# Image loop rewritten as a six-stage software pipeline, second layer norm applied by VectorE

## Chip, cores and metric

One core of one Trainium2 chip. The metric is the device time of one launch in microseconds (us), the median of three runs. Engines: TensorE (PE; its weight loads are PEld), VectorE (DVE), ScalarE (ACT), GpSimd (POOL), and SyncE (SP), which issues the DMAs of the loop.

## The reference, cut to what matters

The input is 32 images of 96 channels by 28x28 positions, all float32.

```python
t0 = x + conv_experts(group_norm(x))   # gate picks 2 of 4 experts; relu(x w1 + b1) w2 + b2, weighted
t1 = t0 + attention(ln(t0))            # per 16-token window: A = fk^T fv * gauss * (1 - lambda), out = q A
y  = t1 + ffn(ln(t1))                  # bitlinear -> gelu -> bitlinear, signs as weights
def bitlinear(x, W, b):                # 5 groups of the batch, each scaled by its own largest |y|
    y = einsum('btc,oc->bto', x, sign(W - mean)) + b
    return clip(y * 128 / (max|y of the group| + 1e-5), -128, 128)
```

The names of the sketch are shortened; attention is linear (no softmax): exp of keys and values gives the feature maps fk and fv, summed into a 96x96 matrix A. The feed-forward part works on 30 of the 32 images (five groups of six).

## The kernel before, in words

Four stages follow one another: statistics and gating (all images resident in SBUF), the image loop, the scales of the first feed-forward layer, and the gelu/second-layer loop, which also writes the result. The change rewrites the second stage.

An image is 96 x 784; it is handled as 7 chunks of 112 tokens. Four PSUM slots S[0] to S[3] of two banks each are shared by everything. Each engine has a program of its own, in a fixed order, and runs it in that order; engines wait for one another by semaphores alone. In the loop a step `i` holds three images: the experts of image i, the attention of image i-1, the first feed-forward layer of image i-2.

TensorE's order in a step (function `step` in the tensor block, L1064): `hidden` 0 and 1 (L1009, 18 matmuls in f16 parts for the three tiles), transposes of t2T(i-2) to tokens (L877), `hidden` 2, transposes of tok1(i-1) to channels, `mix` (L1025, experts' second layer), `kv` (L1070), transposes of the normalised tok2(i-2) to channels, transposes of t1cm(i) to tokens, the sum A of fk and fv (L1173), `ffn_tile` 0, two small matmuls (L1184, L1186), `ffn_tile` 1, a small matmul (L1196), `ffn_tile` 2 (L1032/L1035), and the attention's output (L1202).

VectorE (L1479): statistics of tok2 (`stats`, L1438/L1445), t1cm (L1519), the two feature maps (L1485), the low half of the feed-forward input (`lo`, L1527), the mask Am (L1434), statistics of tok1, three `absmax` over feed-forward tiles (L1457), t2T (L1543), and `apply` (L1451), which normalises tok1 in seven instructions. ScalarE moves PSUM to SBUF (relu L767, tokens L761, xh1T L792, exp L774, big L798) and normalises the next image. GpSimd computes 1/sqrt of the variances (`rstd`, L603 and L609), the low part of the normalised image (`xn_lo`, L583, after it has waited for `xh1_ready`, that is for VectorE's apply), and normalises tok2 (L616). `keep_busy` (L941) are matmuls whose result nobody reads.

In the data of this run both experts' flags agree, so the branch `If(mixed)` takes its `Else` side (L1519) on every image.

Of the kernel before, what the change touches and what calls it, by code (L numbers as in the profile page):

```python
# [7 lines left out]
ALU = mybir.AluOpType  # L8
# [21 lines left out]
P = 128  # L30
# [95 lines left out]
def build(nc, x, gate_w, gate_b, w1, b1, w2, b2, qkv_w, qkv_b, proj_w, proj_b,  # L126
          lk1, lv1, lk2, lv2, W1, fb1, W2, fb2, consts, out):
    with ExitStack() as ctx:
# [24 lines left out]
        w1_raw = sb("w1_raw", [P, TILES, C])  # L153
        w2_raw = sb("w2_raw", [C, E, C])
# [57 lines left out]
        two_ones = sb("two_ones", [PARTS, HALF])  # L212
# [35 lines left out]
        ln_nm = sb("ln_nm", [TOK, CHUNKS])  # L248
# [13 lines left out]
        gel = hT  # L262
# [26 lines left out]
        pool_passed = sem("pool_passed")  # L289
# [54 lines left out]
        xs_loaded = [sem(f"xs_loaded{r}") for r in range(2)]  # L344
        xn_ready = sem("xn_ready")
# [3 lines left out]
        z_ready = sem("z_ready")  # L349
        h_ready = sem("h_ready")  # L350
# [3 lines left out]
        tmp_ready = sem("tmp_ready")  # L354
# [5 lines left out]
        ln_stats = sem("ln_stats")  # L360
# [3 lines left out]
        ln2_negated = sem("ln2_negated")  # L364
# [4 lines left out]
        kv_ready = sem("kv_ready")  # L369
        e_ready = sem("e_ready")  # L370
        f_ready = sem("f_ready")
# [13 lines left out]
        y_ready = sem("y_ready")  # L385
        ymax_done = sem("ymax_done")
# [40 lines left out]

        def piece_of(b):
            return max(n for n, first in enumerate(X_PIECES) if first <= b)
# [5 lines left out]
        def _(sp):  # L435
# [21 lines left out]
            load(fb1r[C:C + PARTS, :], fb1.rearrange("(a n) -> a n", a=1).to_broadcast([PARTS, HID]))  # L457
# [4 lines left out]
            for r in range(2):  # L462
                sp.dma_start(xs[r][:, :], x_bcn[r]).then_inc(xs_loaded[r], 16)

            def load_next(m, r):
                sp.wait_ge(t1_ready, 2 * m + r + 1)
                sp.dma_start(xs[r][:, :], x_bcn[2 * m + r + 2]).then_inc(xs_loaded[r], 16)

            def store_last(m, r):
                i = 2 * m + r  # L470
                sp.wait_ge(t2_ready, i)
                sp.dma_start(out_bcn[i - 1], t2T[1 - r][:, :]).then_inc(t2T_stored[1 - r], 16)

            for m in range(FIRST // 2):
                for r in range(2):
                    load_next(m, r)
                    if m + r > 0:
                        store_last(m, r)
            with sp.Fori(FIRST // 2, LAST // 2 - 1) as m:
                for r in range(2):  # L480
                    load_next(m, r)
                    store_last(m, r)
            for r in range(2):
                store_last(LAST // 2 - 1, r)
            store_last(LAST // 2, 0)
# [38 lines left out]
        def _(pool):  # L524
# [43 lines left out]
            def bf16_parts(src, rows, width, masks):  # L568
                b, h, c = part_b[rows, 0:width], part_h[rows, 0:width], part_c[rows, 0:width]
# [4 lines left out]
            def bf16_rest(dst, rows, width, masks):  # L574
                b, h, c = part_b[rows, 0:width], part_h[rows, 0:width], part_c[rows, 0:width]
# [18 lines left out]
            bf16_parts(fb1r[rows, :], rows, HID, con[rows, K_PART96:K_PART96 + 2])  # L594
            gn_power(4)
            bf16_rest(W1b[rows, :], rows, HID, con[rows, K_PART96:K_PART96 + 2])
# [4 lines left out]
            def rstd(n, b):  # L601
# [3 lines left out]
                if n == 1:  # L605
                    nc.gpsimd.tensor_scalar(ln_nm[:, :], ln_mv[n][:, :, 0], -1.0, None,
                                            ALU.mult).then_inc(ln2_negated, 1)
# [4 lines left out]
            def normalize_2(b):  # L612
                wait_apart(pool, ln_rstd[1], b + 1, pool_passed)
                wait_apart(pool, ln2_negated, b + 1, pool_passed)
                for j in range(CHUNKS):
                    ins = nc.gpsimd.tensor_scalar(tok2[:, j, :], tok2[:, j, :], ln_nm[:, j:j + 1],  # L616
                                                  ln_rs[1][:, j:j + 1], ALU.add, ALU.mult)
                ins.then_inc(xh2_ready, 1)

            def step(m, r, next_=True):  # L620
                i = 2 * m + r
                if next_:
                    pool.wait_ge(xh1_ready, i)
                    xn_rest(1 - r, i + 1)
                if not isinstance(i, int) or i >= 2:
                    rstd(1, i - 2)
                    normalize_2(i - 2)
                rstd(0, i)

            step(0, 0, next_=False)  # L630
            step(0, 1)
            with pool.Fori(1, LAST // 2 - 1) as m:
                for r in range(2):
                    step(m, r)
            step(LAST // 2 - 1, 0)
            step(LAST // 2 - 1, 1, next_=False)
# [3 lines left out]
        def _(act):  # L640
# [99 lines left out]
            def norm_image(m, r, i):  # L740
                resident = isinstance(i, int) and i < FIRST
                if not resident:
                    act.wait_ge(xs_loaded[r], 16 * (m + 1))
                if isinstance(i, int):
                    wait_count(act, z_ready, 3 * (i - 1))
                    wait_count(act, xn_lo_ready, i - 1)
                else:
                    wait_apart(act, z_ready, 3 * (i - 1), act_passed)
                    wait_apart(act, xn_lo_ready, i - 1, act_passed)
                source = x_all[:, i, :] if resident else xs[r][:, :]  # L750
                nc.scalar.activation(xn[r][:, :], source, ACT.Identity, scale=gn_scale[:, bass.ds(i, 1)],
                                     bias=gn_shift[:, bass.ds(i, 1)]).then_inc(xn_ready, 1)
                wait_apart(act, xn_ready, i + 1, act_passed)
                nc.scalar.copy(xn_hi[r][:, :], xn[r][:, :]).then_inc(xn_hi_ready, 1)
# [906 lines left out]
```

## Time and profile before

| what | value |
|---|---|
| time, median of 3 runs (lowest, highest) | 833.73 us (830.05, 836.1) |
| the profiled execution's own time | 830.4 us |
| its span, first to last instruction | 828.6 us |
| mean granted TensorE clock | 0.979 |
| busy: PE, DVE, ACT, POOL | 764.3, 585.8, 476.6, 272.6 us |

The image loop runs from the first `hidden` at 66.97 us to the first gelu at 657.82 us; the last stage, where ScalarE is busy 38.10 of 40 us, takes the rest. In the timeline a row is a run of instructions of one line: start, time to the end of the last, engine, line, operands and in brackets how long the engine idled before and what ended it. An instruction's end overlaps the next one's start, so the time that a piece of work takes up on its engine is read from start to start.

### The profile page before, as it was taken

How to read it: one execution, taken by the hardware profiler on the slowest of the kernel's cores; microseconds unless marked ns; L12 is line 12 of the kernel's file. 1: busy time of each engine (PE TensorE's matmuls, PEld its weight loads, DVE VectorE, ACT ScalarE, POOL GpSimd, SP SyncE). 2: the span in 40 equal slices, each digit the busy share in tenths (PEclk: the TensorE clock that was granted, in tenths of full speed). 3: DMA queues.
4: the chain of work that ended last, by engine and by line, in shares of the span. 5: the costliest groups of instructions: out<-in, count | busy, mean ns of one | idle time of the engine just before them, and what ended most of it. 6: DMA issues, size and time to landing. Idle time of an engine off the chain costs nothing.

```text
span 828.6 us, 15226 instructions
## 1 busy us (share of the span) xinstructions
PE 764.3 (92%) x4663; PEld 508.1 (61%) x4663; DVE 585.8 (71%) x1735; ACT 476.6 (58%) x684; POOL 272.6 (33%) x449
## 2 busy tenths in 40 slices
PE   6798889999999999999999999999999999999991
PEld 3465566667666667666666776666766555555540
DVE  3576467766777766777766677776677468999997
ACT  2453445545555554545554555554553499988981
POOL 1350244454344455334455434345433000000000
PEclk8899999999999999999999999999999999999996
DMA  9860001111111110101100101111100101463333
GB/s 216 198 149 16 22 24 45 31 29 36 36 29 29 44 29 29 44 29 29 43 29 29 44 29 29 32 41 29 34 24 15 32 28 54 150 176 114 119 117 116
DMA packets 20351, 48.62 MB, mean 59 GB/s; under 512 B 4937, under 2 KB 5223, under 8 KB 20327
## 3 DMA queue, kind: packets, MB, share of 16 engines
q1 hardware_dynamic: 19928, 47.72, 20.9%
q10 hardware_dynamic: 399, 0.60, 0.3%
q8 instruction: 13, 0.21, 0.1%
q14 instruction: 11, 0.09, 0.0%
HBM read 29.51 MB, written 18.67 MB: 58 GB/s over the span
## 4 chain that ended last, share of the span: by engine, by line
PE 69%; DVE 10%; ACT 7%; issue 7%; SPq 3%; POOL 2%; DMA 1%; DVEq 0%; ACTq 0%; POOLq 0%
PE slot L1025 15%; PE slot L1009 9%; PE slot L1032 7%; PE slot L1035 6%; PE slot L1173 5%; PE slot L1070 5%; PE slot L1202 5%; PE slot L1233 4%; PE slot L877 4%; PE slot L1237 4%; DVE stage L1485 3%; ACT stage L774 3%; SPq L445 3%; ACT hT L767 2%; PE slot L941 1%
## 5 line engine op out<-in xcount | busy, mean ns | idle before, releaser
L1025 PE MATMUL slot<-hT,w2s 128*96 128x392 f32 x384 | 134.0, 499 | 2.9 <-ACT hT L767 2.3
L774 ACT ACTIVATE stage<-slot,minus_one 112x768 f32<-112x768 f32 x64 | 52.5, 821 | 125.7 <-PE slot L1070 123.3
L767 ACT ACTIVATE hT<-slot,b1c,w_unit 128x784 f32<-128x784 f32 x96 | 93.1, 1006 | 23.0 <-PE slot L1009 23.0
L1519 DVE SCALAR_TENSOR_TENSOR t1cm<-slot,bias,xs 96x784 f32<-96x784 f32 x32 | 32.9, 1029 | 96.9 <-PE slot L1025 96.9
L1025 PEld LDWEIGHTS slot<-hT,w2s 128*96 128x96 f32 x384 | 60.0, 163 | 63.0 <-issue 53.6
L609 POOL TENSOR_TENSOR ln_rs<-ln_ve,pow_half 112x7 f32<-112x7 f32 x62 | 92.8, 1497 | 2.5
L1032 PE MATMUL slot<-big,W1b 99*128 (+1 forms) x360 | 89.5, 329 | 2.7 <-DVE big L1527 0.8
L1035 PE MATMUL slot<-big,W1b 96*128 (+1 forms) x360 | 89.2, 328 | 0.0
L616 POOL TENSOR_SCALAR tok<-tok,ln_nm,ln_rs 112x96 f32<-112x96 f32 x210 | 84.9, 421 | 9.2 <-POOL ln_rs L609 9.2
L583 POOL TENSOR_TENSOR xn_lo<-xn,xn_hi 96x784 f16<-96x784 f32 x32 | 54.4, 1701 | 101.5 <-DVE tok L1451 101.5
L831 ACT ACTIVATE hT<-slot,s 128x784 f32<-128x784 f32 x90 | 80.3, 926 | 6.6 <-DVE stage L1567 6.3
L603 POOL TENSOR_TENSOR ln_ve<-ln_mv,ln_eps 112x7 f32<-112x7 f32 x62 | 12.6, 204 | 216.7 <-DVE ln_mv L1445 216.7
L1457 DVE TENSOR_REDUCE ymax<-slot 128x784 f32 (+1 forms) x90 | 81.2, 959 | 0.0
L1070 PEld LDWEIGHTS slot<-qkvw,xh1T 97*112 97x112 f32 x448 | 73.6, 177 | 10.5 <-issue 9.5
L1485 DVE SCALAR_TENSOR_TENSOR stage<-stage,slot 112x768 f32<-112x768 f32 x64 | 51.8, 850 | 40.0 <-ACT stage L774 40.0
L1070 PE MATMUL slot<-qkvw,xh1T 97*112 97x192 f32 x448 | 78.3, 326 | 0.1
L1438 DVE BATCH_NORM_STATS2 ln_st<-tok 112x6 f32<-112x96 f32 x434 | 74.9, 243 | 4.4 <-ACT tok L761 2.3
L1567 DVE SCALAR_TENSOR_TENSOR stage<-hT,stage 128x784 f16<-128x784 f32 x60 | 56.6, 968 | 14.5 <-ACT stage L840 14.5
L761 ACT COPY tok<-slot 112x672 f32<-112x672 f32 x62 | 44.5, 718 | 24.5 <-PE slot L877 24.5
L1451 DVE TENSOR_SCALAR tok<-tok,ln_mv,ln_rs 112x96 f32<-112x96 f32 x224 | 56.2, 323 | 1.9 <-POOL ln_rs L609 1.9
L1173 PE MATMUL slot<-stage 112*96 112x96 f32 x448 | 46.0, 255 | 12.3 <-DVE stage L1485 12.3
L877 PE MATMUL slot<-con,tok 112*96 112x112 f32 x434 | 52.8, 262 | 4.4 <-POOL tok L616 3.8
(192 smaller groups left out, 1344.6 us busy)
## 6 DMA issues: line engine op xcount, KB each, us to landing
out<-t2T SPq DMA_DIRECT2D x56, 294.0 KB, 2.6
xs<-in_x SPq DMA_DIRECT2D x32, 294.0 KB, 2.9
big<-in_x SPq DMA_DIRECT2D x7, 1176.0 KB, 16.1
xs<-out SPq DMA_DIRECT2D x24, 294.0 KB, 3.3
big<-out SPq DMA_DIRECT2D x1, 1764.0 KB, 11.9
out<-big SPq DMA_DIRECT2D x6, 294.0 KB, 2.6
big<-in_x SPq DMA_DIRECT2D x2, 588.0 KB, 24.3
con<-shape_consts ACTq DMA_DIRECT2D x1, 445.5 KB, 6.1
```

The costliest lines, as they stand in the source:

```text
L609: nc.gpsimd.tensor_tensor(ln_rs[n][:, :], ln_ve[n][:, :], pow_half[0:TOK, 0:CHUNKS], ALU.pow).then_inc(ln_rstd[n], 1)
L616: ins = nc.gpsimd.tensor_scalar(tok2[:, j, :], tok2[:, j, :], ln_nm[:, j:j + 1], ln_rs[1][:, j:j + 1], ALU.add, ALU.mult)
L767: nc.scalar.activation(hT[:, t, :].rearrange("p (a n) -> p a n", a=2), halves(t, P), ACT.Relu, scale=w1_unit[:, t:t + 1], bias=b1c[:, t:t ...
L774: nc.scalar.activation(ekv[:, j0:j0 + n, :], chunks(k, n, 256, 2 * C), ACT.Exp, bias=minus_one[:, :]).then_inc(e_ready, 1)
L831: nc.scalar.activation(gel[:, t, :].rearrange("p (a n) -> p a n", a=2), halves(t, P), ACT.Gelu, scale=s1[:, bass.ds(g, 1)]).then_inc(gelu_ ...
L877: return mm(o, i, ident[0:rows, 0:rows], start=start, stop=True, is_transpose=True, skip_group_check=True)
L1025: ins = mm(S[k][0:C, h, 0:HALF], w2s[:, v, t, :], hT[:, t, h * HALF:(h + 1) * HALF], start=t == 0, stop=t == TILES - 1, skip_group_check=True)
L1032: mm(S[k][:, h, 0:HALF], w, big[:, f, 0, h * HALF:(h + 1) * HALF], start=True, stop=False, skip_group_check=True)
L1035: ins = mm(S[k][:, h, 0:HALF], w[0:C, :], big[0:C, f, 1, h * HALF:(h + 1) * HALF], start=False, stop=True, skip_group_check=True)
L1070: ins = mm(chunks(k, n, 256, 2 * C)[:, j, :], xh1T[:, (j0 + j) * TOK:(j0 + j + 1) * TOK], qkvw[:, C:3 * C], start=True, stop=True, skip_gr ...
L1173: ins = mm(S[3][0:C, 0, 0:C], fkv[:, j, 0:C], fkv[:, j, C:2 * C], start=j == 0, stop=j == CHUNKS - 1)
L1457: V.tensor_reduce(ymax[:, bass.ds(3 * f + t, 1)], halves(k, P), AX.XY, ALU.max, apply_absolute_value=True).then_inc(ymax_done, 1)
```

## The change

The loop's steps now hold six images. A lag tells which image a part of the step works on: hidden layer i, experts' second layer i-1, attention's first half i-2, its second half i-3, tok2 i-4, feed-forward i-5. There are 34 steps after `first_hidden` instead of 32 and one. hT has two buffers, the residual input has its own (xr beside xs), and the setup's raw weights lie in the second hT buffer. GpSimd's `normalize_2` is gone; VectorE does it in the last instructions of its step.

```diff
+        LAG_NORM = LAG_HID = 0
+        LAG_MIX = 1
+        LAG_ATT = 2
+        LAG_OUT = 3
+        LAG_TOK2 = 4
+        LAG_FFN = 5
+        DRAIN = QIMAGES + LAG_FFN
...
@@ GpSimd
-            def normalize_2(b):
...
+            def step(m, r):
+                i, q, _ = at(m, r, LAG_ATT)
+                if exists(i):
+                    rstd(0, i)
+                i, q, _ = at(m, r, LAG_NORM)
+                if exists(i) and not (isinstance(i, int) and i < 2):
+                    xn_rest(q, i)
+                i, q, _ = at(m, r, LAG_TOK2)
+                if exists(i, QIMAGES):
+                    rstd(1, i)
...
@@ TensorE, the order of a step
+                    to_tokens(2, t2T[tok2_q], tok2_in_psum)
...
+                    wait_count(pe, ymax_done[1], ffn)
+                    pe.wait_ge(xh2_ready, ffn + 1)
+                    to_channels(0, tok2, x2p_ready)
...
+                    mix(1, 1, mix_q, 0, 2, 0).then_inc(y_mixed, 1)
...
+                    pe.wait_ge(xh1_ready, att + 1)
                     to_channels(0, tok1, x1T_ready)
...
+                    pe.wait_ge(xn_lo_ready, hid + 1)
+                    wait_count(pe, tok2_ready, tok2_image + 1)
+                    hidden(0, 2, hid_q)
...
+                    kv(0, 0, 0, CH_A)
...
+                    ffn_tile(ffn, 0, 1).then_inc(y_ready[0], 1)
...
+                    to_tokens(2, t1cm[mix_q], tok1_in_psum)
...
+                    kv(1, 3, CH_A, CHUNKS - CH_A)
...
+                    ffn_tile(ffn, 2, 1).then_inc(y_ready[2], 1)
...
+                    hidden(2, 2, hid_q)
...
+                    ffn_tile(ffn, 1, 0).then_inc(y_ready[1], 1)
...
@@ VectorE, the end of a step, the first and the last steps
+                if exists(ffn, QIMAGES):
+                    absmax(ffn, 2, 1)
+                    absmax(ffn, 1, 0)
+                if exists(tok2_image, QIMAGES):
+                    apply(1, tok2, tok2, tok2_image, xh2_ready)
+
+            dve.wait_ge(w0_ready, 1)
+            first_weights_in(1)
+            step(0, 1)
+            first_shares(1)
+            step(1, 0)
+            step(1, 1)
+            first_weights(1)
...
+            for i in range(BATCH, DRAIN):
+                step(i // 2, i % 2)
+            y1_max()
```

Where the instructions stand now, at three places.

TensorE, from the end of one loop step into the next, as changed (L1032 `hidden`, L1055/L1058 `ffn_tile` 1, L1227 the sum A, L900 transposes, L1152/L1153 small matmuls):

```order
L1032 MATMUL slot2<-xn_hi0,w1_lo 128x392 x2
L1055 MATMUL slot0<-big,W1b 128x392 [waits f_ready0]
L1055 MATMUL slot0<-big,W1b 128x392
L1058 MATMUL slot0<-big,W1b 128x392 x2
L1227 MATMUL slot3<-stage 96x96 [waits f_ready1,f_ready0]
L1227 MATMUL slot3<-stage 96x96 x6
L900 MATMUL slot2<-con,t2T1 112x96 [waits t2_ready,h_ready2]
L900 MATMUL slot2<-con,t2T1 112x96 x6
L900 MATMUL slot0<-con,tok2 96x112 [waits xh2_ready,ymax_done1]
L900 MATMUL slot0<-con,tok2 96x112 x6
L1152 MATMUL slot3<-wqT,Am 96x97 [waits am_ready]
```

Between the last feed-forward tile of a step and the transposes of tok2 there now stand the sum A and one set of transposes. Before, the same transposes stood behind `mix` and `kv`, and three tiles came later in the step.

VectorE, the end of a loop step and the start of the next, as changed (L1482 `absmax`, L1476 `apply`, L1547 the mask Am):

```order
L1507 SCALAR_TENSOR_TENSOR stage<-stage,slot3 112x576 [waits e_ready1]
L1482 ISA [waits y_ready2]
L1482 TENSOR_REDUCE ymax<-slot1 128x1
L1482 ISA [waits y_ready1]
L1482 TENSOR_REDUCE ymax<-slot0 128x1
L1476 TENSOR_SCALAR tok2<-tok2,ln_mv1,ln_rs1 112x96 [waits ln2_rstd]
L1476 TENSOR_SCALAR tok2<-tok2,ln_mv1,ln_rs1 112x96 x6
L1547 TENSOR_TENSOR Am<-slot3,gauss 96x96 [waits a_ready]
```

The seven instructions on tok2 stand behind the `absmax` that reads the step's last feed-forward tile, and ahead of the next step's mask and statistics.

GpSimd, one loop step before (first fence) and as changed (second):

```order
L583 TENSOR_TENSOR xn_lo0<-xn0,xn_hi0 96x784 [waits xn_hi_ready]
L603 TENSOR_TENSOR ln_ve1<-ln_mv1,ln_eps 112x7 [waits ln2_mean]
L606 TENSOR_SCALAR ln_nm<-ln_mv1 112x7
L609 TENSOR_TENSOR ln_rs1<-ln_ve1,pow_half 112x7 [waits ln2_var]
L616 TENSOR_SCALAR tok2<-tok2,ln_nm,ln_rs1 112x96 [waits ln2_rstd,ln2_negated]
L616 TENSOR_SCALAR tok2<-tok2,ln_nm,ln_rs1 112x96 x6
L603 TENSOR_TENSOR ln_ve0<-ln_mv0,ln_eps 112x7 [waits ln1_mean]
L609 TENSOR_TENSOR ln_rs0<-ln_ve0,pow_half 112x7 [waits ln1_var]
```

```order
L634 TENSOR_TENSOR ln_ve0<-ln_mv0,ln_eps 112x7 [waits ln1_mean]
L637 TENSOR_TENSOR ln_rs0<-ln_ve0,pow_half 112x7 [waits ln1_var]
L614 TENSOR_TENSOR xn_lo1<-xn1,xn_hi1 96x784 [waits xn_hi_ready]
L634 TENSOR_TENSOR ln_ve1<-ln_mv1,ln_eps 112x7 [waits ln2_mean]
L637 TENSOR_TENSOR ln_rs1<-ln_ve1,pow_half 112x7 [waits ln2_var]
```

xn_lo follows the power of the first norm directly and no longer waits for `xh1_ready`; VectorE's apply on tok1 waits for that same power.

## Rows read from the trace of the kernel before

**Rows 1.** Windows: busy us (instructions) of PE, PEld, DVE, ACT, POOL; granted clock; DMA.
```profile
592.00:632.00 40.00, 39.12 (x239) 26.79 (x237) 27.57 (x106) 20.60 (x28) 17.74 (x29) 1.00 0.10 30
```
**Rows 2.** Timeline of PE, one step: start, us to the end, line, idle before.
```profile
588.04 1.48 PE L1202 MATMUL slot<-xh1T,R 97*96 97x392 f32 x4
589.36 0.50 PE L1009 MATMUL slot<-xn_hi,w_hi 96*128 96x392 f16 x2
...
591.35 0.74 PE L877 MATMUL slot<-con,t2T 96*112 96x96 f32 x7
591.93 0.49 PE L1009 MATMUL slot<-xn_hi,w_hi 96*128 96x392 f16 x2
...
592.92 0.84 PE L877 MATMUL slot<-con,tok 112*96 112x112 f32 x7
593.81 4.19 PE L1025 MATMUL slot<-hT,w2s 128*96 128x392 f32 x12
597.83 2.44 PE L1070 MATMUL slot<-qkvw,xh1T 97*112 97x192 f32 x14
600.11 0.84 PE L877 MATMUL slot<-con,tok 112*96 112x112 f32 x7
600.78 0.74 PE L877 MATMUL slot<-con,t1cm 96*112 96x96 f32 x7
601.94 1.43 PE L1173 MATMUL slot<-stage 112*96 112x96 f32 x14 [0.42 <-DVE stage L1485]
603.38 0.50 PE L1032 MATMUL slot<-big,W1b 99*128 x2
...
604.05 0.33 PE L1184 MATMUL slot<-wqT,Am 96*96 96x97 f32 x2
...
605.89 1.48 PE L1202 MATMUL slot<-xh1T,R 97*96 97x392 f32 x4
```
**Rows 3.** Timeline of DVE in the same step.
```profile
598.04 1.03 DVE L1519 SCALAR_TENSOR_TENSOR t1cm<-slot,bias,xs 96x784 f32<-96x784 f32 x1 [3.21 <-PE slot L1025]
600.27 1.62 DVE L1485 SCALAR_TENSOR_TENSOR stage<-stage,slot 112x768 f32<-112x768 f32 x2 [1.21 <-ACT stage L774]
...
603.41 0.26 DVE L1434 TENSOR_TENSOR Am<-slot,gauss 96x96 f32<-96x96 f32 x1 [0.29 <-PE slot L1173]
...
605.43 2.71 DVE L1457 TENSOR_REDUCE ymax<-slot 128x784 f32 x3
608.05 0.96 DVE L1543 TENSOR_TENSOR t2T<-slot,t1cm 96x784 f32<-96x784 f32 x1
608.93 1.75 DVE L1451 TENSOR_SCALAR tok<-tok,ln_mv,ln_rs 112x96 f32<-112x96 f32 x7
```
**Rows 4.** Timeline of POOL in the same step: the power of the first norm.
```profile
605.88 1.48 POOL L609 TENSOR_TENSOR ln_rs<-ln_ve,pow_half 112x7 f32<-112x7 f32 x1
```
**Rows 5.** Line L583 by itself: shortest, median and longest in ns, first and last start.
```profile
L583 POOL TENSOR_TENSOR xn_lo<-xn,xn_hi x32: 1664/1675/2491, 24.3 to 610.8; 96x784 f16<-96x784 f32 x32
```
**Rows 6.** Timeline of POOL and DVE around the longest L583.
```profile
103.88 0.61 DVE L1334 TENSOR_REDUCE stage<-stage 112x112 f32<-112x448 f32 x1
104.13 2.49 POOL L583 TENSOR_TENSOR xn_lo<-xn,xn_hi 96x784 f16<-96x784 f32 x1 [2.24 <-DVE tok L1451]
...
104.70 0.38 DVE L1336 TENSOR_TENSOR stage<-stage 112x224 f32<-112x224 f32 x1
...
105.89 0.87 DVE L1338 TENSOR_TENSOR stage<-stage 112x112 f32<-112x112 f32 x1
...
107.78 0.27 DVE L1343 TENSOR_TENSOR stage<-stage 112x112 f32<-112x112 f32 x1
```
**Rows 7.** Timeline of PE, two places in the first steps.
```profile
79.66 0.79 PE L877 MATMUL slot<-con,t1cm 96*112 96x96 f32 x7 [1.12 <-DVE t1cm L1519]
...
115.10 1.52 PE L877 MATMUL slot<-con,tok 112*96 112x112 f32 x7 [3.07 <-POOL tok L616]
```
**Rows 8.** Timeline of ACT: the first two gelus.
```profile
657.82 1.89 ACT L831 ACTIVATE hT<-slot,s 128x784 f32<-128x784 f32 x2
```

More of the change, by code:

```diff
@@ L344, in build @@
         xs_loaded = [sem(f"xs_loaded{r}") for r in range(2)]
+        xr_loaded = [sem(f"xr_loaded{r}") for r in range(2)]
         xn_ready = sem("xn_ready")
@@ L479, in _, with load_norm @@
[L479 to L485, printed above, removed]
+                sp.dma_start(xr[r][:, :], x_bcn[r]).then_inc(xr_loaded[r], 16)
+            for r in range(2):
+                sp.dma_start(xs[r][:, :], x_bcn[FIRST + r]).then_inc(xs_loaded[r], 16)
+            def load_norm(m, r):
+                i, q, _ = at(m, r, LAG_NORM)
+                if not isinstance(i, int) or FIRST <= i < BATCH - 2:
+                    sp.wait_ge(xn_ready, i + 1)
+                    sp.dma_start(xs[q][:, :], x_bcn[i + 2]).then_inc(xs_loaded[q], 16)
@@ L486, in _ @@
+            def step(m, r):
+                load_norm(m, r)
+                store_t2(m, r)
+                load_residual(m, r)
+            for i in range(EVEN_FIRST):
+                step(i // 2, i % 2)
+            with sp.Fori(EVEN_FIRST // 2, BATCH // 2 - 1) as m:
+                for r in range(2):
+                    step(m, r)
+            for i in range(BATCH - 2, DRAIN):
+                step(i // 2, i % 2)
             for r in range(2):
@@ L817, in _ @@
+            relu(0, 0, 0, 0)
+            gate_exps(0, 1)
+            relu(0, 0, 2, 2)
+            relu(1, 1, 0, 0)
+            relu(0, 0, 1, 1)
+            relu(1, 1, 1, 2)
+            relu(1, 1, 2, 0)
+            act.wait_ge(signs_ready, 1)
+            nc.scalar.copy(W2last[:, :], W2b[:, TILES - 1, :])
+            gate_exps(1, 0)
+            for i in range(1, EVEN_FIRST):
+                step(i // 2, i % 2)
                 if i == 2:
                     gate_exps(1, 1)
-            with act.Fori(FIRST // 2, LAST // 2 - 1) as m:
+            with act.Fori(EVEN_FIRST // 2, BATCH // 2) as m:
@@ L820, in _ @@
                 for r in range(2):
                     step(m, r)
[L822 to L824 removed]
+            for i in range(BATCH, DRAIN):
+                step(i // 2, i % 2)
             def gelu_tile(g, b, t):
@@ L1170, in step @@
-                if attend:
-                    pe.wait_ge(f_ready, 2 * i)
+                if exists(mixes):
+                    expert_differences(mixes, mix_q, 1)
+                if exists(hid) and not ahead:
+                    pe.wait_ge(xn_lo_ready, hid + 1)
+                    wait_count(pe, tok2_ready, tok2_image + 1)
+                    hidden(0, 2, hid_q)
+                    wait_count(pe, t2_ready, done + 1)
+                    if isinstance(hid, int) and hid == 2:
+                        pe.wait_ge(gate_exp_in, 3)
+                    hidden(1, 3, hid_q)
@@ new lines, in step @@
+                if exists(att):
+                    wait_count(pe, t2_ready, done + 1)
+                    wait_count(pe, h_ready[1], hid + 1 if exists(hid) else BATCH)
+                    kv(1, 3, CH_A, CHUNKS - CH_A)
+                if exists(ffn, QIMAGES):
+                    pe.wait_ge(ymax_done[0], ffn + 1)
+                    ffn_tile(ffn, 2, 1).then_inc(y_ready[2], 1)
+                if exists(hid) and not ahead:
+                    pe.wait_ge(tok1_ready, mixes + 1)
+                    hidden(2, 2, hid_q)
@@ L1556, in _ @@
+            dve.wait_ge(w0_ready, 1)
[5 more added lines that the diff above has]
+            first_weights(1)
+            for i in range(4, EVEN_FIRST):
+                step(i // 2, i % 2)
+            with dve.Fori(EVEN_FIRST // 2, BATCH // 2) as m:
                 for r in range(2):
                     step(m, r)
-            for r in range(2):
-                step(LAST // 2 - 1, r)
-            step(LAST // 2, 0, experts=False, ffn=False, scales=True)
+            for i in range(BATCH, DRAIN):
+                step(i // 2, i % 2)
```

644 lines of the change are left out of this document (296 added, 348 removed).

## The prediction, written before the changed kernel was timed

> **What bounds the kernel now.** I read the windows first, to see which engine is full in the image loop, then one step of TensorE, then VectorE and GpSimd in that step. In 40 us of the loop TensorE is busy for 39.12, VectorE for 27.57, ScalarE for 20.60 [rows 1]: TensorE sets the pace. The step from one attention output to the next takes 605.89 - 588.04 = 17.85 us [rows 2]. It holds two waits: the t1cm transposes take as long as the t2T ones, 0.58 (591.35 to 591.93), so TensorE stood from 601.36 to 601.94, 0.58; the tok transposes take 0.67 (600.11 to 600.78), so it stood 0.22 ahead of the mix at 593.81. The sum A with its wait behind it takes 1.44 (601.94 to 603.38). So some 16.9 to 17.05 us of a step is work, and perfect overlap could win 0.8 to 0.95 us a step, some 25 us in all. That is the prize. The question is whether the new order has a ring of waits that is as long as the old step.
>
> **The steady step after.** The matmuls of an image are the same, so TensorE's work is still 17.05 at most. At a step's start it does the t2T transposes, then the tok2 transposes, which wait for VectorE's apply on tok2, the last thing of the step before. That apply stands behind the absmax of `ffn_tile` 1, and this tile is TensorE's last piece but the sum A. So there is a ring: tok2 transposes, all of TensorE's step to the end of `ffn_tile` 1, absmax, apply, tok2 transposes again.
> - TensorE's part: 17.85 less the two waits (0.58 and 0.22), the sum A (1.44) and the t2T transposes (0.58): 15.03 [rows 2].
> - TensorE to VectorE: t1cm starts at 598.04, 0.21 after the next PE piece started at 597.83 [rows 2, 3].
> - absmax: three from 605.43 to 608.05, 0.87 each. apply: 1.75 to its end [rows 3]; tok2 has the shape of tok1.
> - VectorE to TensorE: the feature maps end at 601.89, PE starts at 601.94: 0.05.
>
> Sum: 15.03 + 0.21 + 0.87 + 1.75 + 0.05 = **17.91 us**. What covers the last four terms (2.88) is only the sum A and the t2T transposes, at most 2.02; the rest is a new wait of 0.9 or more a step. The two old waits do go: kv, transposes and two tiles now stand between the feature maps and their readers. One wait takes the place of two. Queued behind it on TensorE are the small matmuls, the mix and all of the step; ScalarE's St and VectorE's next waits come later by the same time, which the ring contains.
>
> A second ring runs through GpSimd. VectorE goes from the apply on tok2 to the mask Am and the statistics of tok1; from Am's start at 603.41 to the end of the power at 605.88 + 1.48 = 607.36 it is 3.95 [rows 3, 4]. Then apply on tok1 and xn_lo both become free to run. xn_lo, which used to wait for that apply, normally takes 1.68 [rows 5]. If apply goes first and xn_lo after it, xn_lo ends at 3.95 + 0.05 + 1.75 + 1.54 after Am's start (the 1.54 from the next paragraph), and `hidden` 0 waits for it. From `hidden` 0 to the end of `ffn_tile` 1 TensorE's part is 15.03 less the two tok transposes (1.34), the mix (4.02), the output (1.32) and the three small matmuls (603.38 to 605.89 less three tiles of 0.67: 0.50), so 7.85 [rows 2]. Ring: 7.85 + 0.21 + 0.87 + 1.70 (apply, to the next start) + 3.95 + 0.05 + 1.75 + 1.54 + 0.05 = 17.97. Both rings have the length of the old step, so I take **18.0 us** (17.9 to 18.1).
>
> Why 1.54: in the longest xn_lo, 2.49 from 104.13 to 106.62, VectorE ran two-operand operations until 104.70 + 0.38 = 105.08 at their usual length, and then one of 112 columns took 0.87, although one of 224 took 0.38, and ended as xn_lo did [rows 6]. They exclude each other; xn_lo had 1.54 left.
>
> Off the path: VectorE's busy time grows from 12.3 (27.57 x 17.85 / 40) to some 14 us a step, below 18; GpSimd loses its seven operations, which were hidden anyway. SyncE issues one load more per image (xs and xr); its store waits for t2 with the residual's load queued behind, but both loads are used two steps on. ScalarE's xn now heads its step, behind relu 2, and runs while TensorE waits and mixes, before xn_lo is due. These cost nothing while the step is 18 us.
>
> **Filling and draining.** Until the first t1cm transposes at 79.66 [rows 7] nothing that ends last is moved: the hidden layers of image 1 take the place of keep-busy matmuls. Mix 1 ends at 79.66 + 0.58 + 4.02 = 84.3. But `first_shares(1)` now stands ahead of the statistics of image 0: from 103.88 to 107.78 + 0.27 it took 4.2 with a stall of some 0.6 in it [rows 6], so 79.6 + 3.6 = 83.2; statistics and power 3.78 (3.95 less 0.17 for Am), apply 1.85: the tok1 transposes start at 88.9. TensorE has then idled 4.5 us; after 3.07 idle the next transposes took 1.52 where 0.84 is usual [rows 7, 2]. I add 1.4, twice what that set lost. Then 5.5 of PE work, the chain from kv over exp and feature maps to A (600.11 to 601.94, 1.83) and A (1.44): step 2 ends at 99.0. Steps 3 and 4 have no feed-forward and bare chains: 15.0 and 15.6. The tok2 transposes of step 5 start at 99.0 + 30.6 + 0.6 = 130.2. From there to those of step 32 it is 27 steps. The drain (steps 32 and 33 of some 15 us each, as chains lie bare without hidden layers, 10.5 for step 34, 4.3 for the scales, which now begin only after it) I put at 45; the matmuls alone make 28, full steps would make 58; 41 to 49 is my range.
>
> First gelu: 130.2 + 27 x 18.0 + 45 = 661.2, against 657.82 [rows 8]; with a possible slow restart in the drain (0 to 1.5) **+4 us**. At 17.9 and a drain of 41 it is -3, at 18.1 and 49 +10. The last stage is untouched. The profiled execution took 830.4 (span 828.6 and 1.8 around it), so it becomes 834.4. The median of the runs shown, 833.73, is 3.3 higher; on it the sum is **838**, its own range 831 to 843. A change of less than 1% (8.3 us) can't be told from none here.
>
> **The rivals.**
> *GpSimd first, slower.* xn_lo follows the power in GpSimd's own queue, while VectorE's apply must be released by that power. If xn_lo gets in first and apply waits 1.68 for it, apply ends at 3.95 + 1.68 + 1.75 = 7.4 after Am's start; the tok1 transposes would start 6.6 after it (7.18 of PE pieces less their own 0.67 and 0.1 that Am starts earlier). TensorE waits 0.8, the step is 18.7, and 27 steps cost 19 more: 857. It decides where apply is held up by more than 0.8. For it: GpSimd's release is the shorter. Against: VectorE operations that started 0.6 after xn_lo's recorded start were not held up [rows 6]. The Trainium skill, "SBUF — State Buffer", section "SBUF: two separate sides", says that VectorE and GpSimd share a port pair that is an "exclusive lock", and that whoever starts first holds it for the whole instruction. That both exclude each other the trace agrees with; by the rule taken literally GpSimd, first to start, would win here, and the time would be 857. Chance 0.24.
>
> *Small waits add up, slower.* Three chains of nearly one length meet in a step; if each hand-over costs 0.1 more than I read, or the clock falls in some steps, s is 18.25 to 18.4 and the time 844 to 848. It decides from 18.17. Chance 0.18, a quarter of it still within 1%.
>
> *The waits vanish, faster.* If absmax and apply were early enough, TensorE would run its 17.05: 27 x 0.95 = 26 less, 812. Against it stands the order: this absmax can't start before the tile is written. Chance 0.08; a run of before 3 us above the others doesn't help it.
>
> **How the numbers follow.** Forecast 0.50 (nearly all within 1%, 0.02 above). Slower: 0.24 + 0.14 + 0.02 = 0.40; within 1%: 0.48 + 0.04 = 0.52; faster 0.08. The range 830 to 857 leaves out the faster case and the tails.
>
> **What would show it.** In the profile after: steps of 17.9 to 18.1; TensorE idle 0.9 to 1.1 before the tok2 transposes, ended by VectorE's apply; no wait left before A or the mix; xn_lo of 2.5 to 3.3 where apply on tok1 runs (apply first) or an apply stretched by 1.6 (GpSimd first); an idle of over 4 us near 85; gelu from about 661. I am wrong if the tok2 transposes find xh2 ready, or if the step isn't within 17.9 to 18.1.

## The result, and the profile after

The changed kernel takes 863.69 us (862.03 to 865.37), the kernel before 834.78 beside it (830.05 to 836.1): a ratio of 1.0357 (95% interval 1.0307 to 1.0407), 29 us more. The forecast was 838, no change that can be told, with 857 as the upper end of the range.

The profiled execution took 862.03 (span 860.0). Windows of it; the first line answers to [rows 1], the others are the last steps of the image loop and the start of the feed-forward stage:

```profile
592.00:632.00 40.00, 37.06 (x240) 25.98 (x239) 33.73 (x106) 21.06 (x28) 10.00 (x10) 1.00 0.08 23
632.00:672.00 40.00, 31.81 (x180) 22.23 (x178) 29.84 (x110) 9.92 (x17) 6.72 (x8) 0.85 0.06 16
672.00:712.00 40.00, 36.23 (x146) 18.30 (x146) 19.53 (x27) 24.35 (x33) 0.00 (x0) 0.77 0.08 23
```

TensorE is busy 37.06 of 40 instead of 39.12, at full clock (2.4 GHz), so the loop waits more than before; later the granted clock falls to 0.85 and 0.77. In the windows from 632 to 712 of before it was 1.00.

TensorE at the start of two steps (the transposes of tok2, of tok1, of tok2 again; it answers to [rows 2]):

```profile
541.18 0.85 PE L900 MATMUL slot<-con,tok 112*96 112x112 f32 x7 [1.17 <-DVE tok L1476]
...
548.17 0.85 PE L900 MATMUL slot<-con,tok 112*96 112x112 f32 x7 [0.35 <-DVE tok L1476]
...
559.72 0.88 PE L900 MATMUL slot<-con,tok 112*96 112x112 f32 x7 [1.08 <-DVE tok L1476]
```

A step is 559.72 - 541.18 = 18.54 here, and 18.61 in the mean of the 27 from 131.86 (step 5) to 634.25 (step 32). TensorE stands 1.17 and 1.08 us by the rows ahead of the tok2 transposes, about as foreseen (0.9 to 1.1), and again ahead of the tok1 transposes, which was not: the mix's last piece starts at 546.33 and its like takes 1.32 from start to start, so it should have ended at 547.65, 0.5 before they start. (The row shows 0.35, since it counts from the recorded end of the mix, 1.48 after its start. Counted from start to start the two waits at tok2 are 1.33 and 1.24.)

VectorE and GpSimd in that step, answering to [rows 3, 4, 5] (L1482 absmax, L1476 both applies, L637 the power, L614 xn_lo):

```profile
537.39 1.97 DVE L1482 TENSOR_REDUCE ymax<-slot 128x784 f32 x2
539.28 1.76 DVE L1476 TENSOR_SCALAR tok<-tok,ln_mv,ln_rs 112x96 f32<-112x96 f32 x7
540.95 0.25 DVE L1547 TENSOR_TENSOR Am<-slot,gauss 96x96 f32<-96x96 f32 x1
...
543.40 1.48 POOL L637 TENSOR_TENSOR ln_rs<-ln_ve,pow_half 112x7 f32<-112x7 f32 x1
544.85 1.67 POOL L614 TENSOR_TENSOR xn_lo<-xn,xn_hi 96x784 f16<-96x784 f32 x1
...
544.92 3.11 DVE L1476 TENSOR_SCALAR tok<-tok,ln_mv,ln_rs 112x96 f32<-112x96 f32 x7 [0.55 <-POOL ln_rs L637]
```

xn_lo keeps its 1.67; the apply on tok1, released by the same power 0.07 later, takes 3.11 instead of 1.76. A narrow window on VectorE shows which of its seven instructions it is:

```profile
544.92 1.67 DVE L1476 TENSOR_SCALAR tok<-tok,ln_mv,ln_rs 112x96 f32<-112x96 f32 x1 [0.55 <-POOL ln_rs L637]
```

The first one alone lasts until xn_lo ends. That is the mechanism of the rival "GpSimd first".

Filling, answering to [rows 7]: the wait near 85 is there, the slow set behind it too.

```profile
77.32 0.79 PE L900 MATMUL slot<-con,t1cm 96*112 96x96 f32 x7 [1.21 <-DVE t1cm L1535]
87.60 1.54 PE L900 MATMUL slot<-con,tok 112*96 112x112 f32 x7 [5.53 <-DVE tok L1476]
```

TensorE from step 33 to the scales (L1172 the attention output, 1.48 at full clock; L964 nine matmuls on constants), and ScalarE's first gelu, which answers to [rows 8]:

```profile
651.46 0.85 PE L900 MATMUL slot<-con,tok 112*96 112x112 f32 x7 [1.46 <-DVE tok L1476]
...
654.27 2.93 PE L1172 MATMUL slot<-xh1T,R 97*96 97x392 f32 x4 [1.06 <-ACT R L810]
...
669.75 1.09 PE L900 MATMUL slot<-con,tok 112*96 112x112 f32 x7 [2.04 <-DVE tok L1476]
...
672.47 2.93 PE L1172 MATMUL slot<-xh1T,R 97*96 97x392 f32 x4 [0.33 <-ACT R L810]
...
682.15 4.04 PE L964 MATMUL slot<-ones_f,ones_b 128*112 128x512 bf16 x9
```
```profile
688.80 0.92 ACT L854 ACTIVATE hT<-slot,s 128x784 f32<-128x784 f32 x1 [14.87 <-PE slot L1058]
```

Behind these waits the same matmuls take twice as long (2.93 instead of 1.48), which is half clock (1.2 GHz). From the tok2 transposes of step 32 to the first gelu it is 54.55, not 45.

### The profile page after: what moved, and what is told of

Its sections match the earlier page's. It is cut to its first block, busy times and chain, and to the rows that moved or that the text cites. A ratio compares the mean times of both kernels' runs of the same rounds, so it can differ in the third digit from the quotient of the medians.

```text
span 860.0 us, 14841 instructions
## 1 busy us (share of the span) xinstructions
PE 764.2 (89%) x4624; PEld 500.3 (58%) x4624; DVE 680.5 (79%) x1945; ACT 480.5 (56%) x684; POOL 178.1 (21%) x209
## 4 chain that ended last, share of the span: by engine, by line
DVE 34%; PE 31%; issue 9%; ACT 6%; POOL 6%; DVEq 1%; ACTq 0%; POOLq 0%
DVE tok L1476 16%; PE slot L1089 8%; PE slot L1032 7%; PE slot L900 6%; DVE ymax L1482 6%; POOL ln_rs L637 5%; DVE ln_st L1466 4%; PE slot L1055 3%; ACT stage L788 3%; PE slot L1058 2%; DVE stage L1602 2%; DVE ln_mv L1470 2%; PE slot L1265 1%; PE slot L1269 1%; ACT hT L854 1%
## 5 line engine op out<-in xcount | busy, mean ns | idle before, releaser
L1476 DVE TENSOR_SCALAR tok<-tok,ln_mv,ln_rs 112x96 f32<-112x96 f32 x434 | 149.5, 414 | 19.4 <-POOL ln_rs L637 19.4
L1048 PE MATMUL slot<-hT,w2s 128*96 128x392 f32 x384 | 141.7, 493 | 0.0
L1482 DVE TENSOR_REDUCE ymax<-slot 128x784 f32 (+1 forms) x90 | 87.3, 972 | 43.3 <-PE slot L1058 42.6
L782 ACT ACTIVATE hT<-slot,b1c,w_unit 128x784 f32<-128x784 f32 x96 | 96.1, 1004 | 36.3 <-PE slot L1032 36.2
L813 ACT COPY xh1T<-slot 96x784 f32<-96x784 f32 x32 | 25.8, 807 | 160.6 <-PE slot L900 160.6
L900 PE MATMUL slot<-con,tok 112*96 112x112 f32 x434 | 54.9, 268 | 50.4 <-DVE tok L1476 50.4
L1055 PE MATMUL slot<-big,W1b 99*128 (+1 forms) x360 | 91.9, 337 | 1.9 <-DVE ymax L1482 1.1
L637 POOL TENSOR_TENSOR ln_rs<-ln_ve,pow_half 112x7 f32<-112x7 f32 x62 | 91.8, 1480 | 4.8
L1058 PE MATMUL slot<-big,W1b 96*128 (+1 forms) x360 | 91.4, 335 | 0.0
L1089 PE MATMUL slot<-qkvw,xh1T 97*112 97x192 f32 x448 | 85.6, 332 | 1.8 <-ACT xh1T L813 1.8
L900 PEld LDWEIGHTS slot<-con,tok 112*96 112x96 f32 x434 | 41.6, 128 | 76.1 <-issue 40.7
L1507 DVE SCALAR_TENSOR_TENSOR stage<-stage,slot 112x768 f32<-112x768 f32 x64 | 54.3, 850 | 22.8 <-ACT stage L788 22.7
L1055 PEld LDWEIGHTS slot<-big,W1b 99*128 99x128 bf16 x360 | 35.1, 99 | 32.0 <-issue 13.2
L614 POOL TENSOR_TENSOR xn_lo<-xn,xn_hi 96x784 f16<-96x784 f32 x32 | 53.4, 1668 | 0.0
L1265 PE MATMUL slot<-stage,W2b 128*96 128x392 f16 x240 | 46.6, 334 | 5.9 <-DVE stage L1602 2.0
```

The lines of the kernel that those rows point to most:

```text
L637: nc.gpsimd.tensor_tensor(ln_rs[n][:, :], ln_ve[n][:, :], pow_half[0:TOK, 0:CHUNKS], ALU.pow).then_inc(ln_rstd[n], 1)
L782: nc.scalar.activation(hT[q][:, t, :].rearrange("p (a n) -> p a n", a=2), halves(k, P), ACT.Relu, scale=w1_unit[:, t:t + 1], bias=b1c[:, t ...
L900: return mm(o, i, ident[0:rows, 0:rows], start=start, stop=True, is_transpose=True, skip_group_check=True)
L1048: ins = mm(S[k][0:C, h, 0:HALF], w2s[:, v, t, :], hT[q][:, t, h * HALF:(h + 1) * HALF], start=t == first, stop=t == last, skip_group_check ...
L1055: mm(S[k][:, h, 0:HALF], w, big[:, f, 0, h * HALF:(h + 1) * HALF], start=True, stop=False, skip_group_check=True)
L1058: ins = mm(S[k][:, h, 0:HALF], w[0:C, :], big[0:C, f, 1, h * HALF:(h + 1) * HALF], start=False, stop=True, skip_group_check=True)
```

## The experiments

The fill is the loop's first steps, in which not all six images are there yet; the drain is its last ones. Three theories went in. T1: xn_lo holds up the apply on tok1, and the ring through the apply on tok2 comes on top. T2: the longer apply lies in slack, only the ring counts. T3: six images in flight cost by themselves. T4 to T6 came with the later runs. All ratios are to the kernel before, on the same chip. Per profile: the mean step (tok2 transposes of step 5 to step 32, over 27), and the drain (from there to the first gelu):

| run | us | ratio | step | drain |
|---|---|---|---|---|
| the change | 863.7 | 1.0357 | 18.61 | 54.6 |
| e1_xnlo_first | 936.3 | 1.1278 | 21.34 | 53.7 |
| e2_xnlo_waits | 856.6 | 1.0303 | 18.37 | 54.6 |
| e3_apply_mid | 846.6 | 1.0184 | 18.12 | 46.1 |
| e4_pool_norm2 | 817.1 | 0.9846 | 17.14 | 46.2 |
| e5_xnlo_gap | 845.9 | 1.0145 | 18.08 | 53.0 |
| e6_apply_early | 842.4 | 1.0106 | 18.06 | 48.9 |
| e7_busy_drain | 860.0 | 1.0320 | 18.61 | 54.2 |
| e8_pool_gap | 802.7 | 0.9635 | 16.76 | 45.6 |
| e9_busy_all | 856.7 | 1.0312 | 18.61 | 46.2 |
| e10_best | 800.1 | 0.9632 | 16.76 | 43.0 |
| e11_apply_behind_maps | 830.7 | 0.9988 | 17.43 | 54.9 |
| e12_fill_order | 801.4 | 0.9637 | 16.76 | 43.1 |

The start of the loop differs between profiles by some 4 us (the first t1cm transposes from 77.32 to 81.72), so steps and drains tell more than sums.

**e1_xnlo_first.** xn_lo ahead of the power in GpSimd's step.
```diff
+                xn_rest(q, i)          # first in the step
                 rstd(0, i)
-                xn_rest(q, i)
```


> Only GpSimd's order in a step changes: xn_lo ahead of the first norm's power instead of behind it. Theory 1 (GpSimd takes the shared access first and holds up VectorE's apply on tok1, so that TensorE waits 0.5 us a step before the tok1 transposes): apply 1.75 us instead of 3.11, no wait before these transposes, the step 18.6 becomes 18.05, that is 27 x 0.55 = 15 us less than the changed kernel's 863.7: about 849. Theory 2 (the longer apply lies in VectorE's slack and the step is set by absmax and the apply on tok2 alone): apply is shorter, but the wait only moves, the step stays 18.6 and the time 862 to 865.

936.3, interval of the ratio 1.1232 to 1.1323: a miss of both. xn_lo moved into the other apply. VectorE, GpSimd and TensorE there:

```profile
424.21 3.27 DVE L1476 TENSOR_SCALAR tok<-tok,ln_mv,ln_rs 112x96 f32<-112x96 f32 x7
425.51 1.66 POOL L614 TENSOR_TENSOR xn_lo<-xn,xn_hi 96x784 f16<-96x784 f32 x1 [7.39 <-ACT xn_hi L771]
...
427.63 0.95 PE L900 MATMUL slot<-con,tok 112*96 112x112 f32 x7 [2.69 <-DVE tok L1476]
...
429.01 2.80 PE L1048 MATMUL slot<-hT,w2s 128*96 128x392 f32 x4
```

The apply on tok2 had run for 1.3 us when xn_lo came, and still it was held up. A narrow window shows its last two instructions:

```profile
425.40 2.08 DVE L1476 TENSOR_SCALAR tok<-tok,ln_mv,ln_rs 112x96 f32<-112x96 f32 x2
```

Five of the seven took 0.24 each; the sixth, recorded 0.11 ahead of xn_lo, lasts until xn_lo has ended. GpSimd gets into the middle of the series. This apply is the ring itself, and TensorE's wait grows to 2.69. Behind it TensorE runs at half clock (1.2 GHz) for a while: the mix's four matmuls that start at 429.01 take 2.80 instead of 1.48, and the granted clock of 392 to 432 is 0.87. So 1.5 us of hold-up became 2.7 a step. T2's "no effect" falls; the size was in neither theory.

**e2_xnlo_waits.** xn_lo waits for the apply on tok1, as before the change.
```diff
+                    pool.wait_ge(xh1_ready, i - 1)
                     xn_rest(q, i)
```


> xn_lo waits again for the apply on tok1, as in the kernel before the change. Theory 1: apply 1.75 us, xn_lo 1.67 behind it, ends 0.2 to 0.3 after the tok1 transposes, so hidden 0 waits 0.2 to 0.3 where the transposes waited 0.5: step 18.3, about 8 us less than the changed kernel, 856. Theory 2: step 18.6, no change, 862 to 865.

856.6, interval 1.0277 to 1.0329: as T1. The apply on tok1 is back at 1.77, but xn_lo, now behind it, is at the edge of what `hidden` 0 waits for (a wait of 0.15 in some steps, ended by xn_lo): a step of 18.37 shows half of the gain that e5 finds below.

**e3_apply_mid.** The apply on tok2 right behind t1cm, ahead of the first absmax.
```diff
                     convolved(mixes, mix_q, mix_pair, 1)
+                    apply(1, tok2, tok2, tok2_image, xh2_ready)
 ...
-                    apply(1, tok2, tok2, tok2_image, xh2_ready)   # was last
```


> VectorE's apply on tok2 moves from the end of its step to just behind t1cm; GpSimd stays as in the changed kernel. Theory 1: the ring through the last absmax and this apply (15.06 + 0.32 + 0.9 + 1.75 + 0.05) is gone; what is left is VectorE's own chain with the held-up apply on tok1 (3.1 us): about 17.9 a step, 27 x 0.7 = 19 us less, 845. Theory 2: the apply was the whole of it, TensorE is full again, step 17.0 to 17.2, about 40 less, 823.

846.6, interval 1.0145 to 1.0223: the time as T1. No wait is left at tok2, but a new one of 0.8 stands ahead of `ffn_tile` 2, because the first absmax is late:

```profile
549.93 0.51 PE L1055 MATMUL slot<-big,W1b 99*128 x2 [0.79 <-DVE ymax L1482]
```

That the time fits is partly luck: the steps give 13 us (18.61 to 18.12) and not 19, and the drain, which T1 did not count, gives 8.4.

**e4_pool_norm2.** All of the rewrite, but GpSimd normalises tok2 as before.
```diff
-                    apply(1, tok2, tok2, tok2_image, xh2_ready)   # VectorE
...
+                    normalize_2(i)                                # GpSimd, behind rstd(1, i)
```


> The rewritten loop with six images, but GpSimd normalises tok2 as before the change, and VectorE does not. Theory 1: neither ring is left (absmax to the tok2 transposes: 16.3; through xn_lo and apply on tok1: 16.9), TensorE is full, step 17.0 to 17.2, about 40 us less than the changed kernel: 822 to 826, below the 834.8 of the kernel before. Theory 3 (six images in flight cost by themselves, through fill, drain and more hand-overs): step 17.9 or more, 845 or more.

817.1, interval 0.981 to 0.9881: the step is T1's, and T3 falls. The tok2 transposes no longer wait:

```profile
544.89 0.84 PE L915 MATMUL slot<-con,tok 112*96 112x112 f32 x7
...
551.75 0.85 PE L915 MATMUL slot<-con,tok 112*96 112x112 f32 x7 [0.24 <-DVE tok L1491]
```

The time lies below T1's 822; the drain, which T1 did not count, is 8.3 shorter than the change's. Six images in flight are a gain of 1.5%; the norm on VectorE is what made the change slow.

**e5_xnlo_gap.** The change, with xn_lo between the two applies.
```diff
...
+                        pool.wait_ge(xh2_ready, i - LAG_TOK2)    # not in the first steps
+                    xn_rest(q, i)          # now ahead of rstd(0, i)
...
-                    xn_rest(q, i)          # was behind it
```


> The change as it is, but GpSimd computes xn_lo first in its step and waits for the end of VectorE's apply on tok2 before it, so that xn_lo lies between the two applies and falls into neither. Theory T1 (GpSimd's subtraction, started during or just ahead of an apply, holds it up by its own length): the apply on tok1 is back at 1.76 us, TensorE loses the 0.5 us ahead of the tok1 transposes, the steps fall from 18.6 to about 18.1 and the time from 862 to 847-852. Theory T2 (the longer apply lies in slack, the step is set by the apply on tok2 alone): 860-864, steps still 18.5 or more.

845.9, interval 1.0114 to 1.0176: as T1, below its 847. TensorE, VectorE and GpSimd:

```profile
548.30 0.88 PE L902 MATMUL slot<-con,tok 112*96 112x112 f32 x7 [1.08 <-DVE tok L1478]
...
548.40 1.67 POOL L614 TENSOR_TENSOR xn_lo<-xn,xn_hi 96x784 f16<-96x784 f32 x1 [8.00 <-DVE tok L1478]
...
552.14 1.77 DVE L1478 TENSOR_SCALAR tok<-tok,ln_mv,ln_rs 112x96 f32<-112x96 f32 x7 [0.38 <-POOL ln_rs L637]
```

Neither apply is held up, the wait at tok1 is gone, that at tok2 is left: 18.08 a step is the first ring bare (17.91 predicted), and 18.61 - 18.08 = 0.53 a step, 14 us in 27 steps, is the collision.

**e6_apply_early.** The apply on tok2 between the first absmax and the feature maps.
```diff
                     absmax(ffn, 0, 1)
+                    apply(1, tok2, tok2, tok2_image, xh2_ready)
                     feature_map(att, 0, 0, 0, CH_A)
...
-                    apply(1, tok2, tok2, tok2_image, xh2_ready)   # was last
```


> The change as it is, but VectorE applies the second layer norm between the first absmax of its step and the feature maps, not at the end. GpSimd's order is that of the change. Theory T1 (the wait is the place at the end of the step, behind absmaxes that end 2 us after TensorE): no idle time ahead of the tok2 transposes, steps near 17.2 and 818-826, as with the norm on GpSimd; what remains is the held-up apply on tok1, 0.2 us a step. Rival T4 (1.75 us more on VectorE is too much for it wherever it stands, and comes out at another wait, behind the feature maps or the second absmax, as it did 0.8 us a step when the apply stood ahead of the first absmax): steps near 18.0, 838-846.

842.4, interval 1.0074 to 1.0137: as T4. TensorE, the third tile and the tok1 transposes:

```profile
548.46 0.51 PE L1055 MATMUL slot<-big,W1b 99*128 x2 [0.49 <-DVE stage L1507]
...
557.88 0.88 PE L900 MATMUL slot<-con,tok 112*96 112x112 f32 x7 [0.23 <-DVE tok L1476]
```

The wait moved behind the feature maps, which come 1.7 later. The apply on tok1 is still held up (3.10), in e3 too, so the steps of these two runs hold the collision as well.

**e7_busy_drain** and **e9_busy_all.** Matmuls on constants where TensorE stands in steps 33 and 34: e7 ahead of the tok2 transposes, e9 at each wait.
```diff
+                if late:
+                    pe.wait_ge(ymax_done[2], hid - LAG_FFN)
+                    keep_busy(1, 0, 6)                       # e7 and e9
...
                     to_tokens(2, t2T[tok2_q], tok2_in_psum)
...
+                        keep_busy(1, 0, 5)                   # e9, then r_ready
...
+                        keep_busy(1, 0, 6)                   # e9, then xh1_ready
...
+                        keep_busy(1, 0, 4)                   # e9, then xh1T_ready
```


> The change as it is, but in each of the last four steps TensorE first does six matmuls of 512 columns on constants into a slot that nobody reads, where it now stands idle 1.1 to 2 us waiting for the apply on tok2. Theory T5 (TensorE's idle time in the drain is followed by half clock, and the half clock, not the waits themselves, makes the drain 54.5 us instead of 45): the rows of the drain are at full rate (the attention output 1.48 instead of 2.93), the first gelu comes 5-9 us earlier, 853-858. Rival T6 (the drain is long because its steps wait for VectorE, clock or no clock): 860-864.

> The change as it is, with the filling matmuls of the run before this one ahead of the tok2 transposes in the last steps, and now also 4 to 6 of them at each other wait of those steps (ahead of the attention output, of the tok1 transposes, of kv), so that TensorE hardly idles there. In the change the drain's last step ran at half clock and its rows are 5.6 us longer than the same rows of the version with the norm on GpSimd, which were at full clock. Theory T5 (idle time is followed by half clock, and that costs these 5 us): rows at full rate throughout, the drain 48-50 us instead of 54.5, total 856-860. Rival T6 (half clock or not, the waits set the drain): drain 53-55, 861-865.

The edits act in two steps, 33 and 34, not in the last four. e7: 860.0, interval 1.0267 to 1.0373, drain 54.2, as T6 had it; but part of its rows were still at half clock (the last group of matmuls took 4.04 again), so it told nothing yet. e9: 856.7, interval 1.0286 to 1.0339. TensorE in its drain:

```profile
658.54 1.56 PE L1178 MATMUL slot<-xh1T,R 97*96 97x392 f32 x4
...
674.15 1.48 PE L1178 MATMUL slot<-xh1T,R 97*96 97x392 f32 x4
...
680.82 2.11 PE L964 MATMUL slot<-ones_f,ones_b 128*112 128x512 bf16 x9
```

Full clock throughout, and a drain of 46.2 with more matmuls in it than 54.6 had: T5. Filling TensorE's idle time took 8.4 us off the drain. The whole time shows less of it: 856.7 after 863.7, but ratios of 1.0312 and 1.0357, whose intervals overlap. In the profiles e9's loop starts 4.4 later and its first gelu comes 4.1 earlier (684.67).

**e8_pool_gap.** e4, with xn_lo first in GpSimd's step.
```diff
+                xn_rest(q, i)          # first in the step
                 rstd(0, i)
-                xn_rest(q, i)
                 rstd(1, i)
                 normalize_2(i)
```


> The six-image loop with the second layer norm left on GpSimd (817 us in the run before), and xn_lo moved to the start of GpSimd's step, where VectorE has no apply. T1: the apply on tok1 falls from 3.1 to 1.76 us; TensorE waited for it only 0.24 us in every other step, so the steps go from 17.2 to about 17.1 and the time to 812-817. Against T1: no shorter apply, or xn_lo holds up the statistics on tok1 instead, 817-825.

802.7, interval 0.9605 to 0.9665: more than T1 gave it. Windows of TensorE, then VectorE and GpSimd:

```profile
512.00:552.00 40.00, 40.00 (x274) 29.57 (x273) 31.16 (x101) 24.18 (x32) 18.92 (x34) 1.00 0.18 51
```
```profile
551.91 1.67 POOL L617 TENSOR_TENSOR xn_lo<-xn,xn_hi 96x784 f16<-96x784 f32 x1 [3.69 <-ACT xn_hi L786]
...
555.34 1.76 DVE L1491 TENSOR_SCALAR tok<-tok,ln_mv,ln_rs 112x96 f32<-112x96 f32 x7 [0.74 <-POOL ln_rs L643]
```

TensorE never waits: 16.76 is the bare step. e4 lost 0.38 a step (17.14): counted from start to start, its tok1 transposes begin 0.3 to 0.4 late in each step, where the rows show 0.24 in every other one.

**e11_apply_behind_maps.** VectorE's best place found: behind the feature maps, ahead of two absmaxes in the other order, xn_lo first on GpSimd.
```diff
+                    apply(1, tok2, tok2, tok2_image, xh2_ready)
+                    absmax(ffn, 1, 0)
                     absmax(ffn, 2, 1)
-                    absmax(ffn, 1, 0)
-                    apply(1, tok2, tok2, tok2_image, xh2_ready)
```


> VectorE applies the second layer norm, but behind the feature maps and ahead of two absmaxes, whose order is exchanged, and xn_lo is first in GpSimd's step: neither apply is held up, and the tok2 transposes wait for the first of the two absmaxes alone. T1 (the loss is the place and the held-up apply): steps 17.0-17.5, 810-824. T4 (VectorE's 1.75 us more come out at whichever wait follows: statistics and apply on tok1 now start 1.4 us later, ahead of the tok1 transposes): steps 17.6-18.1, 826-842.

830.7, interval 0.9971 to 1.0006. The steps are T1's, 17.43; the time is T4's. Its drain of 54.9 ran at half clock again in part, and 8.7 us less there, as e9 had it, would bring the time into T1's range; no run filled this drain. Wherever VectorE's 1.75 us stood (e3, e5, e6, e11), the step stayed 0.7 to 1.4 above the bare one, in e3 and e6 with some of it due to the held-up apply on tok1.

**e10_best** and **e12_fill_order.** e8 with the gate shares later and the drain filled as in e9, except ahead of the tok2 transposes; e12 takes the power ahead of xn_lo while the loop fills.
```diff
-            first_shares(1)                      # ahead of step 2
...
+                    first_shares(1)              # in step 2, ahead of feature_map
...
 # e12, steps below EVEN_FIRST: xn_rest behind rstd(0, i) and the wait
+                    pool.wait_ge(xh1_ready, new - LAG_ATT + 1)
```


> The best version so far (six images in flight, second layer norm on GpSimd, xn_lo first in GpSimd's step; 802.7) with two more edits: the shares of the second half of the gates are worked out where VectorE waits 7 us for the first exponentials, not ahead of the first statistics, and the drain's waits are filled with matmuls. The first tok1 transposes come 3.5 us earlier and the rows behind them are less slowed (1-1.5): 4-5 us; the drain gains 2-3 where half clock is avoided. 795-799; if the fill's time comes back at a later wait of the filling steps, 800-803.

> The fastest version so far (six images in flight, second layer norm on GpSimd, xn_lo first in GpSimd's step, shares of the second half behind the first t1cm, drain filled; 800.1), with one edit: in the filling steps alone GpSimd takes the power first and xn_lo only when the apply on tok1 is done, since there xn_lo stood 1.0 to 1.7 us ahead of the power in the bare chain from statistics to tok1 transposes. If that chain is what the fill waits for, the first tok1 transposes come 1.7 earlier and three later ones about 1 each: 795-798. If xn_lo behind the apply is then late for the hidden layers, 799-801.

e10: 800.1, interval 0.9606 to 0.9657: the drain gave 2.5 as expected, the fill 0.5 instead of 4 to 5, so its second case. e12: 801.4, interval 0.9612 to 0.9663, 0.4 above its second case. By their ratios e8, e10 and e12 (0.9635, 0.9632, 0.9637) can't be told apart. TensorE in the fill, of e10 and of e12:

```profile
88.93 1.54 PE L915 MATMUL slot<-con,tok 112*96 112x112 f32 x7 [4.04 <-DVE tok L1500]
```
```profile
87.86 0.88 PE L919 MATMUL slot<-con,tok 112*96 112x112 f32 x7 [2.51 <-DVE tok L1504]
89.61 0.84 PE L1051 MATMUL slot<-xn_hi,w_hi 96*128 96x392 f16 x2 [0.88 <-POOL xn_lo L617]
```

In e10 xn_lo stood ahead of the power, in e12 it was late for the hidden layers: two chains end there nearly together, and shortening one left the wait to the other.

## Why the prediction was wrong

From 657.82 the first gelu went to 688.80, 31 us; predicted were 3.4 without the slow restart, 661.2. The 27.6 between:

- **The steady step, 18.0 predicted, 18.61 measured: 16.4 us.** The step that failed is "if apply goes first and xn_lo after it". GpSimd goes first: it starts 0.07 ahead and VectorE's first instruction ends with it, so the tok1 transposes are held up, as the rival "GpSimd first" had it. Its worth is shown by e5: 0.53 a step, 14.3 us. That the rival's step of 18.7 comes so near is partly luck: it put the wait at 0.8 on a ring of 17.91, and they are 0.53 on 18.08. Its time, 857, falls short of 863.7 because it has the drain wrong too. The chance was set wrongly, 0.24, on one look at [rows 6]: there VectorE's operations ran on beside a started xn_lo. There GpSimd was the one held off (2.49 for 1.67), here it never is (1.66 to 1.69 in all 32); what decides between the two when their recorded starts are 0.1 apart, no run here tells. By the Trainium skill, "SBUF — State Buffer", section "SBUF: two separate sides", whichever starts first, GpSimd or a VectorE operation that needs the shared ports, holds them for its whole instruction. The change agrees with it, taken literally: GpSimd started 0.07 ahead and won. In e1 the recorded starts speak against it: VectorE's sixth instruction, recorded 0.11 ahead of xn_lo, was the one held up, and there the measurement decides. That the hold goes by single instructions e1 bears out: a series of seven is broken into.
- **The first ring itself, 17.91 predicted, 18.08 in e5: 2 of the 16.4.** The ring was right in all its members. From the end of `ffn_tile` 1 to its absmax it took 0.32 rather than 0.21 and the absmax 0.90 rather than 0.87.
- **The drain, 45 predicted, 54.55 measured: 9.5 us.** The sum of the chains was about right: with the norm on GpSimd (e8) the drain is 45.6, a part of it at half clock too, and filled (e9) it is 46.2; its parts were not, 17.2, 15.8 and 13.2 in e9 against 15, 15 and 14.8. What failed is "a possible slow restart in the drain (0 to 1.5)". Twice TensorE waited for the apply (1.46 and 2.04), on top of waits for ScalarE, and each time it ran at half clock after it. e9 shows 8.4 us of it.
- **The fill, 1.7 us.** The tok2 transposes of step 5 start at 131.86, not 130.2, and the loop had started 2.3 earlier, so the fill itself took 4.0 more. The idle was 5.5 rather than 4.5: here too xn_lo lay in the apply on tok1, at 84.45 for 3.09 us.

The prediction also overlooked a difference of the two kernels. In its last step the kernel before runs matmuls on constants, and the rewrite has left out all but the last nine of them. These rows are of the kernel before, whose clock stayed at 1.00 in the windows from 632 to 712:

```profile
642.90 2.80 PE L941 MATMUL slot<-ones_f,ones_b 128*112 128x512 bf16 x12
...
650.59 2.10 PE L941 MATMUL slot<-ones_f,ones_b 128*112 128x512 bf16 x9
```

e9 puts such matmuls back.

Right were: one new wait at the tok2 transposes ended by the apply (1.17), the two old waits gone, the stage after the loop untouched. The prediction's own sign of being wrong, a step outside 17.9 to 18.1, was met. TensorE's bare step was put at 17.05 at most, e8 shows 16.76 (the sum A, counted as 1.44 with its wait, takes 1.19), so the prize was 29 us. The rival "the waits vanish" (812) comes near what the rewrite does without its move of the norm: 817.1 (e4), and 802.7 with xn_lo moved too (e8). The move of the norm by itself cost 46.6 us (e4 to the change, 43 by the ratios).

## What to carry to other kernels

When one engine's work is given to another, look for the ring in which the receiver's last operation and the first use of the next round lie, and add what the two engines do to each other when one event releases both. Two operations that exclude each other belong in different gaps of the step, by order, not by luck: here that alone was worth 2.1% of the time in either version, some 18 us by the ratios (e5 against the change, e8 against e4), of which the steps show 14 and 10. Short waits in a stage that is thin on matmuls cost more than their length where the clock falls behind them, and in this drain matmuls on constants were cheaper than the bare wait. When a loop is rewritten, look where the old one had such matmuls.

## What was not expected of the hardware

- GpSimd's subtraction goes ahead of VectorE's apply even when it comes 1.3 us after the apply's start (e1: 3.27 instead of 1.76).
- Waits of 2.4 to 2.7 us in each step were followed by half clock in all but the first two of 26 steps (e1, granted 0.87 to 0.92 in the windows from 192 to 672), while waits of 1.1 to 1.2 in each step left it at 1.00 (the change, e5). In the drain waits of 1 to 2 us close together, with few matmuls between, were followed by half clock; with the waits filled it stayed at 1.00 in the window 632 to 672 of e9, where the change had 0.85.
